# Attention values turned through DRAM instead of on TensorE, with the projections in a new order

## What is computed

```
q = einsum('bnd,hed->bhne', xf, Wq)
k = einsum('bnd,hed->bhne', xf, Wk)
v = einsum('bnd,hed->bhne', xf, Wv)
s = einsum('bhqe,bhke->bhqk', q, k) * scale
s = where(mask, s, finfo.min)
p = softmax(s, axis=-1)
out = einsum('bhqk,bhke->bhqe', p, v)
```

## Time and profile before

| | |
|---|---|
| median of 3 runs | 1245.13 us (1244.61 to 1247.14) |
| profiled execution | 1246.36 us, of it span 1244.4 us |
| TensorE busy | 1216.4 us, 98% |
| VectorE, ScalarE, GpSimd busy | 690.4, 475.1 and 641.5 us |
| mean granted clock of TensorE | 0.997 |

### The profile page before, as it was taken

One profiled execution on the slowest core, in us unless ns is written; L12 is line 12 of the kernel. 1 busy time (PEld: TensorE's weight loads), 2 busy tenths in 40 slices (PEclk: granted clock), 3 DMA queues, 4 the chain that ended last, 5 costly groups with the idle time before them and its releaser, 6 DMA issues.

```text
span 1244.4 us, 19555 instructions
## 1 busy us (share of the span) xinstructions
PE 1216.4 (98%) x6768; PEld 975.0 (78%) x6768; DVE 690.4 (55%) x1434; ACT 475.1 (38%) x1229; POOL 641.5 (52%) x726
## 2 busy tenths in 40 slices
PE   6999999999999999999999999999999999889998
PEld 4788896478888888888888878777887787668887
DVE  7534444775665433666452578756347776476212
ACT  3611141034645320656341164644206555243212
POOL 4633389256565567555546655555665556464000
PEclk9999999999999999999999999999999999999999
DMA  5211124025564643454645356557535565620012
GB/s 185 84 46 48 34 56 117 8 65 160 154 169 137 184 134 97 127 177 128 185 136 166 86 160 212 180 160 223 168 102 151 175 209 156 205 60 1 29 40 68
DMA packets 129376, 155.03 MB, mean 125 GB/s; under 512 B 30080, under 2 KB 84000, under 8 KB 129280
## 3 DMA queue, kind: packets, MB, share of 16 engines
q1 hardware_dynamic: 118976, 146.92, 39.7%
q10 hardware_dynamic: 10304, 6.88, 1.8%
HBM read 111.81 MB, written 37.75 MB: 120 GB/s over the span
## 4 chain that ended last, share of the span: by engine, by line
PE 89%; DVE 5%; ACT 2%; issue 1%; DMA 1%; SPq 1%; POOL 0%; ACTq 0%; DVEq 0%; POOLq 0%
PE PS L1137 53%; PE PS L682 7%; PE PS L1758 7%; PE PS L1183 4%; PE PS L960 3%; PE PS L969 2%; PE PS L975 2%; PE PS L1227 2%; PE PS L1216 2%; PE PS L1775 2%; PE PS L1247 2%; PE PS L665 1%; PE PS L1197 1%; DVE bst L257 1%; PE PS L700 1%
## 5 line engine op out<-in xcount | busy, mean ns | idle before, releaser
L1137 PE MATMUL PS<-XB,w_hi 128*128 128x512 f32 x1024 | 340.5, 397 | 1.2 <-POOL w_lo L228 1.2
L226 POOL CAST w_hi<-w_raw 128x512 fp32r<-128x512 f32 x195 | 124.2, 637 | 307.5 <-PE PS L1137 213.0
L228 POOL TENSOR_TENSOR w_lo<-w_raw,w_hi 128x512 fp32r<-128x512 f32 x195 | 256.1, 1313 | 15.6
L1137 PEld LDWEIGHTS PS<-XB,w_hi 128*128 128x128 f32 x1024 | 192.2, 188 | 47.1 <-issue 5.0
L1137 PE MATMUL PS<-XB,w_lo 128*128 128x512 f32 x512 | 200.2, 391 | 0.0
L1137 PE MATMUL PS<-XB,part 128*128 128x512 f32 x768 | 190.3, 394 | 0.0
L1137 PEld LDWEIGHTS PS<-XB,part 128*128 128x128 f32 x768 | 141.9, 188 | 32.2 <-issue 2.3
L1373 ACT ACTIVATE part<-PS,nmax 128x256 f32<-128x256 f32 (+1 forms) x256 | 112.2, 443 | 141.6 <-DVE nmax L1485 93.2
L1383 ACT ACTIVATE part<-part,prec 128x256 f32<-128x256 f32 (+1 forms) x256 | 105.8, 476 | 27.7 <-DVE prec L1500 27.7
L228 POOL TENSOR_TENSOR part<-part,part 128x512 fp32r<-128x512 f32 x85 | 111.5, 1312 | 6.8
L1137 PE MATMUL PS<-part,w_hi 128*128 128x512 f32 x344 | 112.9, 395 | 1.5 <-DVE part L1544 1.5
(11 more groups left out here) (136 smaller groups left out, 1884.0 us busy)
## 6 DMA issues: line engine op xcount, KB each, us to landing
w_raw<-in_w SPq DMA_DIRECT2D x187, 256.0 KB, 2.8
part<-in_w SPq DMA_DIRECT2D x85, 256.0 KB, 2.8
turned<-part SPq DMA_DIRECT2D x128, 128.0 KB, 2.9
part<-turned SPq DMA_DIRECT2D x32, 512.0 KB, 5.0
turned<-part SPq DMA_DIRECT2D x128, 96.0 KB, 2.5
part<-turned SPq DMA_DIRECT2D x32, 384.0 KB, 4.0
strips<-part ACTq DMA_DIRECT2D x16, 256.0 KB, 2.7
out_x<-xT SPq DMA_DIRECT2D x16, 256.0 KB, 2.1
```

The costliest lines, as they stand in the source:

```text
L226: pool.tensor_copy(hi, raw).then_inc(w_hi_done, 1)
L228: pool.tensor_tensor(lo, raw, hi.bitcast(F32), ALU.subtract).then_inc(w_ready, 1)
L1137: m = nc.tensor.matmul(PS[:, bank, :], wt[:, (c % 4) * P:(c % 4) * P + P], rhs(hl, c), start=c == k == 0, stop=c == CK - 1 and k == 2)
```

## The change

The values no longer pass TensorE. VectorE turns 32x32 blocks of them straight from PSUM into vB, SP writes these to DRAM with four DMAs and reads them back turned with one, and ScalarE rearranges them into v (take_v). The bias of the values in layer 2 is added to the output instead. TensorE's order of an item becomes: scores, relative products, keys of i+1, queries of i+2, values of i, attend(i-1); at j = 0 attend(i-1) stands before the values, and the output blocks behind them. The probabilities of an item are written with four DMAs of twice the size, and read back with two of 512 runs each in place of two of 128. evac_relative moves ahead of the first two normalize, evac_o and rest_of_o to the start of the next item but one (at j = 0 also behind the item), sum_relative's first two quarters to the end of the item before, and evac_q and rest_of_q behind the norm work. At the end six output blocks are open side by side, the last attends come between their halves, and build_m is spread over all blocks. Cut to its core:

```diff
             if i + 1 < ITEMS:
                 take_block(i + 1, "K")
+            if i + 2 < ITEMS:
+                take_block(i + 2, "Q")
             take_block(i, "V", range(0 if i else 1, 2))
             if s and j == 0:
                 for o in range(CK):
                     take((s - 1, "O", o), STAGES[s - 1][0], "O", o)
-            if i + 2 < ITEMS:
-                take_block(i + 2, "Q")
...
-        def turn_values(i):
-            pe.wait_ge(v_evac, i + 1)
...
-            for tt in range(4):
-                m = nc.tensor.transpose(PS[:, turned_bank(i), tt * P:tt * P + P], vT[:, tt * P:tt * P + P], ident[:, :])
-            m.then_inc(v_tr, 1)
...
         for i in range(1, LAST - 1):
             score_block(i)
             project(i + 1, "K", range(CK))
-            attend(i - 1, 0)
-            attend(i - 1, 1)
-            project(i, "V", range(CK))
-            if i % PAIRS == 0:
+            project(i + 2, "Q", range(CK))
+            if i % PAIRS:
+                project(i, "V", range(CK))
+                attend(i - 1, 0)
+                attend(i - 1, 1)
+            else:
+                attend(i - 1, 0)
+                attend(i - 1, 1)
+                project(i, "V", range(CK))
                 s = i // PAIRS - 1
-                out_block(s, 0, range(CK))
...
+                for o in range(CK):
                     out_block(s, o, range(CK))
...
+        def take_v(i):
+
+            act.wait_ge(v_in, 16 * (i + 1))
             if i:
-                act.wait_ge(v_tr, i)
...
+                act.wait_ge(o_done, 2 * i)
+            dst = v.rearrange("p t (b c) -> p t b c", b=4)
+            nc.scalar.activation(dst, vB.rearrange("p (b t c) -> p t b c", b=4, t=4), ACT.Copy).then_inc(v_ready, 1)
...
+            if i >= 2 and j != 1:
+                evac_o(i - 2)
             exps(i, 0)
             exps(i, 1)
+            evac_relative(i + 1)
             normalize(i, 0)
             normalize(i, 1)
-            evac_relative(i + 1)
             exps(i, 2)
             normalize(i, 2)
+            if i == LAST:
+                take_v(i - 1)
             exps(i, 3)
-            if i and j == 0:
-                evac_o(i - 1)
             normalize(i, 3)
             evac_k(i + 1)
-            if j:
-                evac_o(i - 1)
-            evac_v(i)
+            if 0 < i < LAST:
+                take_v(i - 1)
...
+            evac_q(i + 2)
+            if i and j == 0:
+                evac_o(i - 1)
...
+        def turn_values(i):
+
+            product_done(dve, (i, "V"))
             if i:
-                dve.wait_ge(o_done, 2 * i)
...
+                dve.wait_ge(v_ready, i)
+            src = PS[:, bank_of(i, "V"), :].rearrange("p (t q c) -> p t q c", t=4, q=4)
+            dst = vB.rearrange("p (q t c) -> p t q c", q=4, t=4)
+            nc.vector.transpose(dst, src).then_inc(v_turned, 1)
...
+            rest_of_q(i + 2)
+            if i and j == 0:
                 rest_of_o(i - 1)
...
+            sum_relative(i + 1, 0)
+            sum_relative(i + 1, 1)
+            if i < LAST:
+                turn_values(i)
...
+    def values_to_dram(sp, i):
+
+        sp.wait_ge(v_turned, i + 1)
+        if i >= 2:
+            sp.wait_ge(v_in, 16 * (i - 1))
+        for b in range(4):
+            to = bass.AP(values.tensor, (i % 2) * P * 4 * P + P * b, [[4 * P, 32], [32 * 4 * P, 4], [1, P]])
+            sp.dma_start(to, vB[32 * b:32 * b + 32, :].rearrange("p (q r) -> p q r", q=4)).then_inc(v_out, 16)
+
+    def values_from_dram(sp, i):
+        sp.wait_ge(v_out, 64 * (i + 1))
+        sp.dma_start(vB, values[i % 2, :, :]).then_inc(v_in, 16)
...
+    STRIPS_AT = [slots[(i, "K"), 0] + (7 if i < LAST else 6) for i in range(ITEMS)]
+    PROBS_AT = [slots[(i + 1, "K"), 0] + 9 for i in range(LAST)] + [slots[(3, "O", 5), 0]]
+    BACK_AT = [PROBS_AT[i] + 2 for i in range(LAST - 1)] + [PROBS_AT[LAST - 1]]
...
+                if i < LAST and n == BACK_AT[i]:
+                    values_to_dram(sp, i)
                     probs_from_dram(sp, i, 0)
...
                     probs_from_dram(sp, i, 1)
+                    values_from_dram(sp, i)
...
-    M_AFTER = {(0, 1): (), (1, 1): (0, 1), (2, 1): (2, 3), (3, 0): (4,), (3, 1): (5, 6),
-               (4, 0): (7,), (4, 1): (8, 9), (5, 0): (10, 11), (5, 1): (12,), (6, 0): (13,), (6, 1): (14,), (7, 0): (15,), (7, 1): ()}
...
+    M_AFTER = {(0, 1): (0, 1), (1, 1): (2, 3), (2, 1): (4,), (3, 1): (5, 6), (4, 1): (7, 8), (5, 1): (9,),
+               (6, 0): (10, 11), (6, 1): (12, 13), (7, 0): (14, 15), (7, 1): ()}
```

## The result

The changed kernel takes 1238.24 us (median of 14 runs, 1235.92 to 1243.08), the kernel before beside it 1244.92 (1242.43 to 1247.14): a ratio of 0.995 [0.9939, 0.9961], 6.7 us less. Forecast were 18.8 us less.

What follows compares the result with a forecast made beforehand. TensorE, busy for 98% of the span, was taken as the bound. Terms -14.1 - 1.1 - 2 + 4.5 + 3 - 9.1 = -18.8 us took the median from 1245.1 to 1226 us; range 1215 to 1240.

Steps and rivals of the forecast that it cites:

- transposes gone: All 32 items: the value transposes leave TensorE's path, 0.44 us each, 14.1 us saved.
- items 22 and 23: Layer 2: attend's wait for turned probabilities in these two items goes, 1.1 us saved.
- order of the products: TensorE's item, over 29 items: new order saves a change of product kind; gain 2 us, bounds loss 1 to gain 6.
- new waits at j = 0: Items 8, 16, 24: attend waits for take_v on ScalarE, 0.3, 2.6 and 1.6 us late; 4.5 us lost, at most 8.
- j = 1 and behind: Items 17 to 20 and 25 to 28: late softmax delays queries and next relative products; 3 us lost, bounds 0 to 8.
- the end: Item 30's scores to layer 3: of 12.6 us lost to waits and clock, 9.1 us gained; bounds 3 to 12.6.
- some 2 us late against the values' end: Items with j = 1 to 4: turn_values waits behind two VectorE sums; rest_of_o and next maxima have 2 us to spare.
- regains 0.3 an item: Layer 2, j = 1 to 4: VectorE's 21.5 us round against a 21.8 us item slowly recovers the delay, gone afterwards.
- a round of over 22 us: Sign the prediction is wrong: VectorE's round longer than 22 us, so the delay grows from item to item.
- The other sign: Sign the prediction is wrong: the clock falls in the middle of a stage.
- Rival B: Transposes go but the end gives nothing, small products' evacuations and SP's queue carrying its waits; 1235 us, chance 0.13.

Runs made afterwards that it cites:

- e5: Kernel before with its four value transposes per item left out of TensorE's queue, all waits around them kept; 1232.2 us, ratio 0.9889.
- e3: Changed kernel with ScalarE rearranging the returned values ahead of the softmax's fourth exponential at j = 0 and in item 30; 1228.35 us, ratio 0.9872.
- e2: Changed kernel with VectorE turning the values ahead of the two relative-embedding sums in items with j = 1 to 4; 1228.31 us, ratio 0.9858.
- e8: Changed kernel with the edits of e1, e2 and e3 together; 1211.46 us, ratio 0.9726.
- e1: Changed kernel with chunk statistics aggregated between output blocks and group statistics moved into the next item; 1227.03 us, ratio 0.985.
- e7: Changed kernel with queries of items 8, 16 and 24, and their evacuation and rest, moved back behind the output blocks; 1235.63 us, ratio 0.9921.
- e11: e8 with attend(i-1) ahead of values(i) at j = 1 to 7, take_v staying behind the keys' evacuation; 1271.4 us, ratio 1.0211.
- e9: Changed kernel with a stage's norm work spread over five items instead of four; 1249.21 us, ratio 1.0035.
- e4: Changed kernel with 11 unused products added ahead of the relative products in items 18 and 26, filling the wait; 1236.97 us, ratio 0.9937.
- e6: Changed kernel with attend(i-1) back ahead of values(i) and take_v ahead of the fourth exponential, in every item; 1237.09 us, ratio 0.9927.

## Why the prediction was wrong

The direction was right and the time lies inside the range, 1.8 us under its upper end, but the gain is a third of the forecast: 6.7 us of 18.8. Term by term, in the profiled execution, whose layer 3 took 0.1 us longer besides (what the undisturbed items save is the table's before less the undisturbed lengths: 19.6 and 21.28 us an item, 64.71, 65.02):

| step | forecast | measured | from |
|---|---|---|---|
| transposes gone | -14.1 | -16 | e5, 0.50 an item |
| items 22 and 23 | -1.1 | -1.1 | both 21.28 |
| order of the products | -2 | -11.1 | 3.9 in items 1 to 15, 6.0 in 17 to 23 and 25 to 29, 1.0 in 16 and 24, 0.2 ahead of item 1 |
| new waits at j = 0 | +4.5 | +6.2 | changed less e3: 0.08, 3.8, 2.3 |
| j = 1 and behind | +3 | +18.5 | 157.83 less 7 x 21.28; 116.01 less 5 x 21.28 |
| the end | -9.1 | -4.9 | 84.07 against 89.93, less two items' transposes |
| sum | -18.8 | -8.4 | |

**Right.** The transposes were on the path at their full length. Attend's waits of items 16 and 24 came where they were put, 2.21 us each against 2.6 and 1.6; `evac_relative` held the queries up by 0.52 and 0.59 against 0.4; the four waits of the small products are 0.48, 0.40, 0.52 and 0.53 and POOL's is 0.20, 2.1 us against 3.5. The maxima of item 17 start 4.5 us in, against 4.7. SP was not the bound: reads of the turned probabilities take 0.53 us to issue, and TensorE waited for weights once in this part, those 0.20 us. By the rule of the Trainium skill ("VectorE: DVE Perf Modes", "The three transpose paths") weighed in the prediction, the return trip would have lasted several items by its estimate; the trace disagrees: a write of the values landed in 2.3 us and the read in 4.7.

**The step that failed.** It is the term +3 for the items behind j = 0, measured as +18.5, and in it the sentence on `turn_values` "some 2 us late against the values' end". It named whom that holds up: `rest_of_o`, the next maxima, SP. It left out `relative`, which waits for `v_turned` because half of what it writes lies in the values' bank, and which stands not a block of products behind but directly behind the next scores. The wait is in the whole diff, as a renamed semaphore (the cut one shows only where it is raised): `relative` waited for `v_evac` before, ScalarE's early copy, and now for VectorE's last step. e2 moved that one step: of the four waits of 2.50, 1.70, 2.50 and 0.96 us were left 1.30, none, 2.03 and none.

**The step that was too small for a reason of its own.** "VectorE's round, some 21.5 us, against a new item of 21.8, regains 0.3 an item." The round was about right, 21.5 in the mean of e8 and 21.8 in items 19 and 20 of e1, but the item is 21.28, because the order gave five times what I had priced. The sign of the difference is what decided: the delay grew instead of decaying. A gain on the bound engine was paid back where another engine's round was 0.2 to 0.5 us longer. As what would make the prediction wrong I had named a round of over 22 us; it was enough that the item got shorter. The other sign that I had named did come, the clock falling in the middle of a stage (at 722.9, 948.2 and 996.0 us). e1 and e7 show that the late start doesn't explain the waits alone, e2 that the place of the turn doesn't; e8, which changes both, leaves 0.25 of the 7.7 us, with the norm work as it was.

**The price of a wait.** I counted the clock in the account of the end (3.6 us) and not in the new waits. In items 1 to 29 the changed kernel has 20.5 us at the lower clock (3.4, 6.8, 6.8, 3.4; the 3.4 in item 30 are the end's), where the kernel before has none; at half a microsecond for each that is 10.2 of the 24.7 us that the new waits cost. The waits themselves are 13.2 (7.7 of `relative`, 1.1 of the queries, 4.4 of attend), and most of the remaining 1.3, as an estimate, is what each restart costs: 0.26 of waiting made e1's items 0.53 us longer.

**The end.** -4.9 instead of -9.1, and one wait accounts for most of it. In item 30 there are no queries, so attend(29) stands directly behind the values and is due 14.0 us in, before ScalarE's `take_v`; I had looked only at attend(30). It cost 2.2 us and 1.7 at the lower clock. Without it (e3) the stretch takes 80.6 us, and "about 80" was forecast.

**The order.** The forecast took the lower part of its bounds, 2 us, and the 11.1 measured lie far above their upper end of 6. A change of kind costs 0.22 to 0.30 us as measured, a little over the 0.1 to 0.2 assumed, but attend directly ahead of the scores costs nothing extra, and the 0.17 us by which the relative products were held up in every item of layer 2 was not seen at all: it lies in the earlier trace rows ahead of and inside their 1.52 us (1.26 now), and was read as theirs.

Rival B named the wrong place: the end gave most of what was expected, had it not been for attend(29), and the middle gave back what B put there. The time, 1238, is close to B's 1235 for another reason, and since the upper end of the range was made from B, it is luck that the time lies inside.

## What to carry to other kernels

When a step moves to another engine, follow every wait on its old semaphore to its new one, and for each ask when the waiter is due and what now stands ahead of the release in the new engine's queue; banks shared by two uses are where this hides. When the bound engine gets faster, compare its new period with the next engine's period under its heaviest load, not its average: at 56% mean load VectorE's round was longer than TensorE's item in the items with norm work. And price a wait on TensorE at its length, about 0.3 us for the restart, and 1.6 us or 3.4 more when the clock falls behind it; here removing three causes of short waits (e8) was worth four times the change itself.

## What the runs showed of the hardware

The clock falls after waits far shorter than I had thought, and not after all of them. It stayed up behind 2.21 us in item 24 and fell behind the same 2.21 in item 16 and behind 0.96 in item 28 of the changed kernel; in e11 it fell behind six waits of 3.6 us and not behind two others. The lower level lasts 3.4 or 6.8 us (13.7 once, in e9), and costs about half of that: 1.62 us for 3.4 in e1 and 1.60 in e11. The Trainium skill ("TensorE: Matmul & The Clock Gate", "Why this matters for your kernels") warns of gaps between bursts of products, longer ones than most of these; the traces show that much shorter ones, down to 0.93 us in item 19 of e4, can be enough. What decides in the single case stays open: no run here separates it. The time of such a kernel scatters with it: 1235.92 to 1243.08 us in 14 runs of the changed kernel, whose mean clock goes from 0.992 to 0.988 in the same order at its two ends, and only 3.2 us in the four runs of e8, whose clock is 0.999 or 1.0.

Going over from one form of product to another costs 0.22 to 0.30 us at the head of a block of 512 columns (e6). The Trainium skill ("TensorEngine Tiling (Array Packing)", "Key Properties") says that changing the tiling mode drains the engine; attend, scores and the projections are of three modes, and the trace agrees in that each change has a price, with this number.

The two sums on VectorE took 1.27 us in the changed kernel's item 17 and 2.38 in e7's, and the first copy of the coefficients 1.09 and 0.17. Both work within the on-chip memory while POOL does. Whether POOL is the cause was not tried; a tail of VectorE can be a microsecond longer from one run to the next.
